# Moving two PE steps between the fourth and fifth query unit of the pairs that run alone, and a weight rounding behind the probabilities

## The reference

```python
xn = _layernorm(x)
x = x + mla(xn) + experts_top4(xn)      # layer 0: 16 heads, causal softmax
xn = _layernorm(x)
x = x + sparsemax_attention(xn) + ffn(xn)
# ffn: rmsnorm, grouped softmax attention, rmsnorm, experts_top2
```

## Time and profile before

| | us |
|---|---|
| median of three runs | 3135.06 |
| the profiled execution | 3136.48 |
| its span (first to last instruction) | 3134.7 |

### The profile page before, as it was taken

One profiled execution on the slowest core, in us unless ns is written; L12 is line 12 of the kernel. 1 busy time (PEld: TensorE's weight loads), 2 busy tenths in 40 slices (PEclk: granted clock), 3 DMA queues, 4 the chain that ended last, 5 costly groups with the idle time before them and its releaser, 6 DMA issues. The chain is left out here.

```text
span 3134.7 us, 61375 instructions
## 1 busy us (share of the span) xinstructions
PE 2818.1 (90%) x20990; PEld 2279.4 (73%) x20990; DVE 2185.9 (70%) x6269; ACT 1613.6 (51%) x3388; POOL 1504.1 (48%) x2213
## 2 busy tenths in 40 slices
PE   5887799999999999978988898898799999999986
PEld 4555478889899889846666666666588888888864
DVE  6878578788778788767777777766645555454576
ACT  3544344544454445545655555665455555555554
POOL 4768643443343354385556666322233333332487
PEclk8877699999999999999999999999899999999999
DMA  3556478788888878422333434210466666676356
GB/s 83 198 206 214 174 265 310 278 287 309 287 290 306 299 284 306 180 41 54 96 98 104 108 104 109 93 68 23 162 206 216 220 208 221 204 241 204 122 97 126
DMA packets 212009, 580.15 MB, mean 185 GB/s; under 512 B 24616, under 2 KB 146416, under 8 KB 167408
## 3 DMA queue, kind: packets, MB, share of 16 engines
q1 hardware_dynamic: 172528, 523.82, 47.7%
q0 software_dynamic: 36864, 51.14, 7.9%
q10 hardware_dynamic: 2304, 1.21, 0.1%
HBM read 450.14 MB, written 125.96 MB: 184 GB/s over the span
## 5 line engine op out<-in xcount | busy, mean ns | idle before, releaser
L480 PE MATMUL bank<-xh,gu 128*128 128x256 f32 x3520 | 673.5, 291 | 35.1 <-DVE gc L1653 26.3
L1138 POOL TENSOR_TENSOR al<-t,ah 128x512 fp32r<-128x512 f32 x220 | 283.4, 1288 | 878.1 <-ACT ah L1374 878.1
L480 PEld LDWEIGHTS bank<-xh,gu 128*128 128x128 f32 x3520 | 513.8, 190 | 58.9 <-issue 55.1
L523 PE MATMUL bank<-masks_bf,ident_bf 128*128 128x128 bf16 x1896 | 432.4, 251 | 136.2 <-ACT ksT L1458 43.3
L1839 DVE TENSOR_REDUCE st<-bank 128x1 f32<-128x512 f32 (+3 forms) x1024 | 422.2, 481 | 163.1 <-PE bank L541 155.5
L1471 ACT ACTIVATE pt<-bank 128x512 f32<-128x512 f32 (+1 forms) x1152 | 512.9, 542 | 38.4 <-PE bank L544 25.5
L523 PEld LDWEIGHTS bank<-masks_bf,ident_bf 128*128 128x128 bf16 x1896 | 170.2, 99 | 358.3 <-DVE st L1839 93.0
L1479 ACT ACTIVATE oT<-bank 128x512 f32<-128x512 f32 x192 | 114.5, 597 | 598.6 <-PE bank L620 580.1
L541 PE MATMUL bank<-ksT,qsT 128*128 128x512 f32 (+3 forms) x1536 | 413.1, 370 | 5.6 <-DVE top L1837 2.9
L544 PE MATMUL bank<-qaT,ksT 128*128 128x512 f32 (+3 forms) x1536 | 397.9, 369 | 0.0
L480 PE MATMUL bank<-xl,gu 128*128 128x256 f32 x1760 | 352.1, 282 | 0.0
(11 more groups left out here) (254 smaller groups left out, 5272.1 us busy)
## 6 DMA issues: line engine op xcount, KB each, us to landing
gu<-wu_scratch SPq DMA_DIRECT2D x110, 1032.0 KB, 5.2
gu<-wu_scratch SPq DMA_DIRECT2D x110, 1024.0 KB, 7.5
dn<-wd_scratch SPq DMA_DIRECT2D x110, 1024.0 KB, 6.7
xs<-xs_scratch SPq DMA_DIRECT2D x110, 264.0 KB, 4.4
ys_scratch<-yb SPq DMA_DIRECT2D x110, 256.0 KB, 6.9
raw<-in_gu SPq DMA_DIRECT2D x16, 1024.0 KB
wu_scratch<-hi SPq DMA_DIRECT2D x16, 1024.0 KB
wu_scratch<-lo SPq DMA_DIRECT2D x16, 1024.0 KB
```

What stands on the lines that cost most here:

```text
L480: mm = pe.matmul(bank[:, TS * h:TS * (h + 1)], gu[:, col:col + P], x[s % 2][:, TS * k:TS * (k + 1)], start=(n == 0), stop=(n == len(terms) ...
L523: return pe.matmul(S.bank((which, G, u))[:, diag:diag + P * len(unit)], ident_bf[:, :], masks_bf[:, side, 0:len(unit), :].rearrange("p n k ...
L1138: pool.tensor_tensor(em["al"][s % 2][:, m, :], em["t"][g % 2][:, :], em["ah"][s % 2][:, m, :].bitcast(F32), ALU.subtract).then_inc(al_read ...
```

## The change

In pairs alone:

- PE: the query scores of the next pair are asked for in two parts, units 0 to 3 (`GAP = 4`) and units 4 and 5. Between them stand `route_bias` and, where the next batch is mla, `project`. They stood at the end of the pair.
- ACT: `take_projected` for mla moves from behind the probabilities to before O; `first_high` moves from before O to behind the probabilities.
- DVE: `first_low` moves behind `heads_out` and `route_place`; `add_bias` moves ahead of `heads_out`.

```diff
+GAP = 4
@@ PE, pair_alone
-                        scores("q", G + 1, range(NU))
+                        scores("q", G + 1, range(GAP))
+                    if routes(G, 3):
+                        route_bias((G - 3) // 2)
+                    if n + 1 < nb and kinds[n + 1] == "mla" and 1 <= p <= NT:
+                        project(n + 1, p - 1)
+                    if G + 1 < steps:
+                        scores("q", G + 1, range(GAP, NU))
...
-                    if routes(G, 3):
-                        route_bias((G - 3) // 2)
-                    if n + 1 < nb and kinds[n + 1] != "gqa" and 1 <= p <= NT:
+                    if n + 1 < nb and kinds[n + 1] == "spm" and 1 <= p <= NT:
                         project(n + 1, p - 1)
@@ ACT, pair_alone
-                    if routes(G, 1):
-                        first_high((G - 1) // 2)
                     if is_at(n + 1, "gqa") and 2 <= p <= NT + 1:
                         take_projected(n + 1, p - 2)
+                    if n + 1 < nb and kinds[n + 1] == "mla" and 1 <= p <= NT:
+                        take_projected(n + 1, p - 1)
...
                     probabilities(G, range(NU))
+                    if routes(G, 1):
+                        first_high((G - 1) // 2)
...
-                    if n + 1 < nb and kinds[n + 1] != "gqa" and 1 <= p <= NT:
+                    if n + 1 < nb and kinds[n + 1] == "spm" and 1 <= p <= NT:
                         take_projected(n + 1, p - 1)
@@ DVE, pair_alone
                         route_weigh((G - 2) // 2)
-                        first_low((G - 2) // 2)
...
+                    if routes(G, 3):
+                        add_bias((G - 3) // 2)
                     if G:
                         heads_out(G - 1)
...
                         route_place((G - 2) // 2)
+                    if routes(G, 2):
+                        first_low((G - 2) // 2)
                     if routes(G, 1):
                         route_select((G - 1) // 2)
-                    if routes(G, 3):
-                        add_bias((G - 3) // 2)
```

## The result

The changed kernel took 3190.85 us (median; 3188.96 to 3193.26), the kernel before 3134.39 beside it: ratio 1.0175, interval 1.016 to 1.019. That is 56 us more by the medians and 55 by the ratio. The profiled execution has a span of 3187.9 us against 3134.7, so 53.2 us are to be found in the two traces.

A forecast was written before the change was run, and what follows sets the result against it. PE's order, with DVE a link, was taken to pace gqa, and mutual waits the first stage. Terms 28 (gqa) + 4 + 2 (spm) + 5 (mla) - 2 (first stage) = 37 us on 3135 gave 3172 us, range 3145 to 3198.

The forecast's parts named there:

- The effect outside the title: Pairs alone: masks of units 0 to 3 come behind all four products; DVE starts 1.17 us after the first, before 0.62.
- 0.58 us a pair: Pairs alone: outputs come 0.58 us later where DVE's start waits for PE; gqa 28 us more, bounds 20 and 33.
- The other late stages: Late masks outside gqa: mla alone 5 us more, spm alone before the experts 4, spm after them 2.
- The first stage: First 21 pairs: gains and costs of the moved steps and late masks sum to -2 us, bounds -25 and +18.
- the +2.5 for the masks: First stage: the five pairs without a gap step pay 0.58 us less their cover, +2.5 us.
- The roundings: First stage, ACT: first-half roundings no longer stand ahead of the exponents, -4 us.
- DVE's add_bias ahead of heads_out waits for products that are long done: nothing.: DVE, first stage: moving the bias addition ahead of the head outputs costs nothing.
- The waits for heads_out go from PE: First stage: PE's 16.2 us of waits for heads_out and the bias go; a quarter counted, -4 us.
- A: Rival: all PE waits in the first stage go (-25), masks cost 20 in gqa and 9 elsewhere; 3139 us, chance 0.12.
- B: Rival: the masks cost nothing, four-unit form not taken or PE catches up behind O; 3133 us, chance 0.07.
- C: Rival: added PE idle time also costs clock, 26 us more over 40 gqa pairs; 3198 us, chance 0.07.
- D: Rival: first stage worse by its upper bound (+18), POOL's chain and DVE both delayed; 3192 us, chance 0.08.

The follow-up runs named there:

- e2: The kernel before with its six query units asked for as four and two, nothing between, so only the masks' place changes: 3163.35 us, ratio 1.0152.
- e9: e2 with one mask meant to come early; the edit acted only in pairs with experts, so pairs alone are as in e2: ratio 1.0148.
- e1: The changed kernel with the masks ahead of the products again in pairs alone, all moved steps kept: 3111.91 us, ratio 0.9998 to the kernel before.
- e7: The kernel before with the rounding of the raw weights alone moved, ACT's behind the probabilities, DVE's behind the places: ratio 0.9999.
- e3: e1 with the projection ahead of the bias products in the gap: 3102.66 us, ratio 0.9965 to the kernel before on the first chip.
- e12: e3 unchanged, run again on the third chip: ratio 1.0020 to the kernel before.
- e4: The kernel before, masks first, with the last pair's outputs between the fourth and fifth query unit in pairs alone: 3133.89 us, ratio 1.0062.

## Why the prediction was right, and where it was not

**The effect outside the title: right.** Late masks were named as the main cost, and e2 shows that they make 1.52% by themselves (e9, the same in pairs alone, 1.48% on another chip). With the masks first, e1, the rest of the change makes 0.9998. In the timeline the first mask starts 0.95 us after the first product (estimate 0.65 + 0.26 = 0.91) and DVE 0.33 us behind it (0.26 taken), 1.28 us in all, where I had 1.17.

**0.58 us a pair: right for the start, a little small for the pair.** For the eight pairs of a gqa batch, before to after: the start of the first maximum, counted from the copy to `qaT` (median over the eight batches), and the length of the pair from one such copy to the next (mean):

| pair | start of maxima | shift | pair longer by |
|---|---|---|---|
| 0 | 3.64 to 3.35 | -0.29 | -0.24 |
| 1 | 2.93 to 3.56 | 0.63 | 0.57 |
| 2 | 4.12 to 4.72 | 0.60 | 0.63 |
| 3 | 1.06 to 1.63 | 0.57 | 0.60 |
| 4 | 0.94 to 1.47 | 0.53 | 0.32 |
| 5 | 2.70 to 3.78 | 1.08 | 0.85 |
| 6 | 2.06 to 2.74 | 0.68 | 0.65 |
| 7 | 0.66 to 1.34 | 0.68 | 0.77 |

The sum of a batch is 4.15 us, eight batches 33.2; I had 28, and 33 as the upper bound. The five pairs whose maxima wait for PE are 1, 2, 5, 6 and 7. They pay 0.69 us on average instead of 0.58, 27.8 us for 23.2, most of the surplus in pairs 5 and 7. The two that I took as partly covered (3 and 4, DVE going straight on, as at 1824.96) pay 7.4 us for 6: pair 3 had so little cover that it pays in full, pair 4 half. Pair 0, behind the row statistics, hides it, as said, and is even 1.9 us shorter in all batches together. The 1 us that I took off for a chain on DVE was not there. So the term mis-sized is the price of a waiting pair, and less so the cover of the others. In pair 5 the first product also comes 0.2 us later (in e2 as well); why was not followed up.

**The other late stages.** mla 5 forecast, 5.0 measured; spm 4 and 6.5; the end 2 and 4.0. Sum of the three: 11 forecast, 15.5 measured. At the end I let POOL's chain of gathers take over from about 3011 us. The changed kernel has +4.0 there and e2 +5.1, but the unchanged kernel had +3.1 in its second profile, so these can't be told from my 2. In spm, e2 has +4.2, my 4. The changed kernel's further 2.3 us go with a lower granted clock, 0.86 against 0.91 before and in e2, and with PE busy for 114.7 us instead of 109.1.

**The first stage: not settled.** Forecast -2 (bounds -25 and +18), measured +4.9 from one pair of profiles, and +2.4 in pair 21 behind it. The same kernel before gives 368.9 and 364.1 us in two profiles, so 4.9 can't be told from -2. Timed, the change without its late masks (e1) is at -0.6 us (-3.7 to +2.2) in all, on the first chip. My terms without the +2.5 for the masks give -4.5 for it, just outside. That the -2 comes near is in part luck, since its single terms don't stand so well:

- The roundings, -4 forecast: e7 shows 0 within 3.5 us. The microsecond or so a pair that I allowed for `stack` beside the second-half rounding does not show either. In the first stage before, 11 of the 147 operations of `stack` lie beside a rounding on DVE and take 0.71 us on average, the others 0.32 (its operation of L1186 alone has a median of 0.45 and at most 1.32); in e7 there are 4 such. All 147 together take 51.8 us before and 51.3 in e7.
- "DVE's add_bias ahead of heads_out waits for products that are long done: nothing." This step failed. I asked what DVE waits for, and not who waits for DVE's reading of the bank. With the bias products in the gap, O takes a bias bank, and PE waited 7.64 and 6.99 us for it in two pairs of the changed kernel, 23.1 us in all in e1's first stage. I had even written that Ta no longer reuses a bias bank (right: it waits no more), without asking which step does now. e3 takes O's wait away and is 9 us faster than e1 on the same chip. On the third chip the order of e3 (e12) is 0.2% slower than the kernel before; e1 was not run there.
- "The waits for heads_out go from PE": the 14.1 us are 0.3 us in the changed kernel. POOL's stack holds the transposes up 12.7 us (18.4 before). These waits did go, but new ones of O stand in the same stage, 22.5 us.

**The rivals.** A (the first stage pays for everything) and B (the masks cost nothing) fall with e2 and with the stage table. C (lost clock) falls for the gqa stage: the granted clock is 0.98 before and after, with 0.64 us of wait in a pair as above. The Trainium skill's warning about PE's idle gaps (TensorE: Matmul & The Clock Gate, "HAM oscillation — how this bites in real kernels") was rightly not given more than C's chance: waits of this length left the granted clock of that stage where it was. In the two short stages of the changed kernel it is lower than before, 0.90 against 0.95 in mla alone and 0.86 against 0.91 in spm alone. The late masks don't explain that, since e2 has 0.93 and 0.91 there, and e1 has 0.92 and 0.88 without being slower. D (first stage +18) falls with the stage table and e1. The measured time alone would have spoken for D: 3190.85 us lies next to its 3192, and 19 us above my 3172.

**The total.** 37 forecast, 53 between the two profiles, 16 too few: 5 from gqa, 4.5 from the rest behind the experts, 7 from the first stage. The part of the masks is sure (e2: 47 us, interval 42 to 53). The rest, some 8 us, is not: e1 shows no cost of the moved steps on the first chip, but e3 and e12 are the same kernel and differ by 0.55% of the kernel before between two chips, so the moved steps may well cost a few us where the change was timed. e1 was run on one chip only.

## What to carry to other kernels

A condition that compares a count with a number of buffers can change its answer when work is merely cut in two: look for every test that a new call with a smaller range passes. Where a consumer works through a batch without a gap, look at its first start: here a start 0.6 us later made most pairs 0.6 us longer, and 0.21 us less of the producer's work in between was worth nothing. A late end of that batch seems to cost as well (e4). Whoever moves a step in a shared ring of banks must ask who gets the bank next, and when its reader frees it, not only what the moved step waits for.

## What the runs showed of the hardware

The same kernel (e3 and e12) has a first stage of 335 us on one chip and 372 on another, while all other stages agree within 3 us. e2 and e9, which are the same in this stage, have 350 and 378. The kernel before stood at 3113 us on the first chip and at 3137 on the two others. Each chip was used in one session only, so chip and session are not separated. Between e3 and e12 most of the difference lies in five pairs: 7.2 us in pair 7, 4.7 in 9, 10.2 in 15, 4.5 in 16 and 8.3 in 17. Between e2 and e9 it is 9.6, 11.2 and 12.0 in pairs 7, 9 and 15. PE is also busy 13 us longer in e12's first stage, at a granted clock of 0.81 against 0.83; the rest is waits. In pair 15 DVE waited ahead of the router's logits, first e12 (the profile names no engine of this core as the releaser), then e3:

```profile
331.31 0.19 DVE L2044 TENSOR_TENSOR rt<-bank,rb 128x32 f32<-128x32 f32 x1 [7.42 <-remote]
```

```profile
305.32 0.19 DVE L2044 TENSOR_TENSOR rt<-bank,rb 128x32 f32<-128x32 f32 x1 [0.53 <-PE bank L695]
```

The product that it reads had run on PE from 320.67 to 322.52 in e12, nearly 9 us earlier. What held DVE there is open: it was not tried, and the trace does not show it. The practical consequence is plain: of an edit in this stage, a few tenths of a per cent on one chip need a second chip before they are believed.
